# Expert products in scaled fp16 parts made once in the first stage, and single tiles in the pairs' form

## The chip, the core and the metric

One core of one Trainium2 chip runs the whole program. The metric is the device time of one execution in microseconds (us); less is better. The engines are named as the profile names them: PE is the matrix engine (PEld its weight loads), DVE the vector engine, ACT the scalar engine, POOL the general engine, SP the engine that issues most transfers.

## The reference

Four residual blocks over x (4 x 1024 tokens of 256 numbers): cross attention, a mixture of experts with a shared network, a second cross attention, and a gated network with integer weights. The change touches the second block alone:

```python
logits = (xt @ gate_w.T + gate_b).astype(jnp.float32)
scores = jax.nn.softmax(logits, axis=-1)
top_w, top_i = jax.lax.top_k(scores, TOPK)          # 2 of 8 experts for each token
...
def expert(w1e, b1e, w3e, b3e, w2e, b2e):           # each matrix is 256 x 256
    h = jax.nn.silu(xt @ w1e.T + b1e) * (xt @ w3e.T + b3e)
    return h @ w2e.T + b2e
outs = jax.vmap(expert)(w1, b1, w3, b3, w2, b2)
y = jnp.einsum('etd,te->td', outs, gate_dense)
z = jax.nn.silu(xt @ ws1.T + bs1) * (xt @ ws3.T + bs3) @ ws2.T + bs2
```

## The kernel before

**Three stages.** Stage 1 takes the tokens in 8 groups of 512. Its `step(g)` (g from 1 to 7, one on each engine) interleaves the first attention of group g with the shared network and the routing of group f = g - 1, and POOL scatters the normalised rows to DRAM by expert (`rows_by_expert`). Stage 2 (the expert loop) takes the scattered rows in 40 units: 31 pairs (256 rows) and 9 singles (128 rows), in the order of `KINDS`: 13 pairs, then nine times pair, pair, single. Stage 3 gathers the experts' results and does the rest of the shared network, the second attention and the last network. Nothing is scheduled by a planner: every engine runs the order written in its block, and semaphores tie them.

**Products in parts.** A product of full precision is three matmuls (`three`, L1306): high x high, high x low, low x high, where high is the value copied to the narrow type `F32R` on ACT and low is the rest, subtracted on DVE. The three stand in the profile at L1308, L1309 and L1310.

**Stage 2 before.** SP loads for each unit the two first matrices of its expert (`wraw`, 512 KB, L470), ACT copies them to `wph` (`weights_high`, L985) and DVE subtracts `wpl` (`weights_low`, L2272): once per unit, 40 times. The second matrices of all 8 experts (`w2h`, `w2l`) are split in stage 1 instead: in each step `expert_high(g)` on ACT (128x512, the last of the step; two of them in step 1) and `expert_low(g)` on DVE. PE transposes the unit's rows (`tx`, L1649), makes the hidden layer (`hidden`: for a pair the weights are stationary and 24 matmuls of 256 columns run; for a single the rows are stationary, 6 matmuls of 512 columns, and the hidden layer must be transposed back by `th`, L1686), and multiplies by the second matrix (`outp`, 12 or 6 matmuls of 256 columns). The order on PE for unit u is `hidden(u)`, `outp(u - 2)`, `th(u - 1)` where that is a single, `tx(u + 2)`. ACT does `silu_of`, `out_copy`, `rows_high`, `high_of`; DVE `gated`, `rows_low`, `hidden_low_of`; POOL adds the bias; SP stores.

**Stage 1, one step, in order.** PE: `up(f,0)`, `probs_t(g)`, setup products of the second attention (steps 2 to 6; in step 3 `queries`), `up(f,1)`, `values(g)`, `gate(f)`, `up(f,2)`, `gate_back`, `t1(g+1)`, `up(f,3)`, `scores(g+1)` (waits for both `n1T` copies), `rank`, `down(f)` first part, `t2(g)`, `down(f)` second part. ACT: `silu(f,0)`, `pt_copy(g)` (writes `probsT`, for which `values` waits), `silu(f,1)`, `hidden_high(f,0)`, `logit_copy`, `silu(f,2)`, `hidden_high(f,1)`, `t1_copy(g+1)` (writes `n1T`), `hidden_high(f,2)`, `ln2_apply(g)`, `silu(f,3)`, `hidden_high(f,3)`, `route_exp`, `t2_copy(g)` (`n2Th`, for which the next `up` waits), `softmax(g+1)`, `expert_high(g)`. DVE: `hidden(f,0)`, `residual1`, `ln2_stats`, `hidden(f,1)`, `route_a`, `hidden(f,2)`, `route_b`, `hidden(f,3)`, `route_d`, `row_max(g+1)`, `t2_low(g)`, `shared_out`, `ln1_stats`, `route_c`, `expert_low(g)`.

## Time and profile before

| | before |
|---|---|
| median of 3 runs | 618.06 us (617.78 to 622.72) |
| the profiled execution, its own time | 616.33 us |
| its span in the profile | 614.5 us |
| PE busy | 569.9 us, 93% |
| DVE busy | 453.1 us, 74% |
| ACT busy | 377.6 us, 61% |
| POOL busy | 253.5 us, 41% |
| granted PE clock, mean | 0.985 of full |
| moved by DMA | 93.15 MB, mean 152 GB/s |

The profile is one execution, and its 616.33 us stands 1.73 us under the median; 1.83 us of it lie outside the span. Matmuls are pipelined, so the duration of one (0.28 us for 256 columns) is not what it costs: the distance between two starts is. The chain of waits that ended last is PE for 66% of the span and DVE for 17%.

### The profile page before, as it was taken

How to read it: one execution, taken by the hardware profiler on the slowest of the kernel's cores; microseconds unless marked ns; L12 is line 12 of the kernel's file. 1: busy time of each engine (PE TensorE's matmuls, PEld its weight loads, DVE VectorE, ACT ScalarE, POOL GpSimd, SP SyncE). 2: the span in 40 equal slices, each digit the busy share in tenths (PEclk: the TensorE clock that was granted, in tenths of full speed). 3: DMA queues.
4: the chain of work that ended last, by engine and by line, in shares of the span. 5: the costliest groups of instructions: out<-in, count | busy, mean ns of one | idle time of the engine just before them, and what ended most of it. 6: DMA issues, size and time to landing. Idle time of an engine off the chain costs nothing.

```text
span 614.5 us, 12817 instructions
## 1 busy us (share of the span) xinstructions
PE 569.9 (93%) x3906; PEld 469.0 (76%) x3906; DVE 453.1 (74%) x1246; ACT 377.6 (61%) x729; POOL 253.5 (41%) x284
## 2 busy tenths in 40 slices
PE   7889999998967999999999999799889989999997
PEld 7788888886747999999999988476646646655654
DVE  5887887886644877778788863477888798877755
ACT  5576777873534777777687663155574674684643
POOL 4445665553540134454343345577533640410100
PEclk9899999998997999999999999999999999999999
DMA  7334664441238868887978717542212240200000
GB/s 213 120 112 143 206 207 161 153 166 58 104 137 249 284 223 287 276 248 249 311 225 291 240 67 285 186 157 69 62 35 70 85 138 35 69 2 35 34 36 35
DMA packets 46005, 93.15 MB, mean 152 GB/s; under 512 B 6686, under 2 KB 15978, under 8 KB 45682
## 3 DMA queue, kind: packets, MB, share of 16 engines
q1 hardware_dynamic: 37868, 74.34, 35.5%
q0 software_dynamic: 7344, 17.97, 9.7%
q8 instruction: 33, 0.54, 0.4%
q14 instruction: 34, 0.28, 0.1%
q10 hardware_dynamic: 726, 0.02, 0.1%
HBM read 61.32 MB, written 32.17 MB: 152 GB/s over the span
## 4 chain that ended last, share of the span: by engine, by line
PE 66%; DVE 17%; issue 6%; ACT 5%; another core or an unknown queue 4%; POOL 1%; DMA 0%; ACTq 0%; DVEq 0%; POOLq 0%
PE bank L1310 13%; PE bank L1308 13%; PE bank L1309 12%; PE bank L1805 6%; DVE st L2381 3%; PE bank L1649 2%; PE bank L1826 2%; PE bank L1827 2%; PE bank L1277 2%; PE bank L1294 2%; DVE g3l L2458 2%; DVE xa L2372 2%; DVE sl L2453 2%; PE bank L1266 1%
## 5 line engine op out<-in xcount | busy, mean ns | idle before, releaser
L625 POOL DMA_INDIRECT rows_by_expert<-n,pos x64 | 64.6, 1010 | 53.4 <-DVE pos L2109 36.9
L674 POOL TENSOR_TENSOR yg<-yg,b 128x512 f32<-128x512 f32 x31 | 44.7, 1443 | 98.6 <-ACT yg L798 98.6
L722 POOL DMA_INDIRECT yr<-expert_out,out_row x64 | 64.7, 1011 | 28.3 <-issue 19.7
L1308 PE MATMUL bank<-xTh,wph 128*128 128x256 f32 x248 | 73.8, 297 | 1.7 <-DVE xTl L2300 1.2
L1805 PE MATMUL bank<-m4Th,wint 128*128 128x512 f16 x192 | 69.0, 380 | 5.3 <-DVE sl L2453 3.3
L1310 PE MATMUL bank<-xTh,wpl 128*128 128x256 f32 x248 | 71.2, 287 | 0.0
L1309 PE MATMUL bank<-xTl,wph 128*128 128x256 f32 x248 | 71.1, 287 | 0.0
L1805 PE MATMUL bank<-m4Tl,wint 128*128 128x512 f16 x192 | 68.8, 379 | 0.0
L2274 DVE TENSOR_TENSOR wpl<-wraw,wph 128x1024 fp32r<-128x1024 f32 x40 | 49.0, 1225 | 12.8 <-ACT wph L798 12.6
L798 ACT ACTIVATE wph<-wraw 128x1024 fp32r<-128x1024 f32 x40 | 42.3, 1058 | 16.3 <-PE bank L1310 9.6
L1308 PEld LDWEIGHTS bank<-xTh,wph 128*128 128x128 f32 x248 | 48.5, 196 | 2.1 <-issue 1.4
L2453 DVE SCALAR_TENSOR_TENSOR sl<-bank,sl 128x512 f32<-128x512 f32 x48 | 33.0, 688 | 22.5 <-ACT sl L1113 22.4
L1309 PEld LDWEIGHTS bank<-xTl,wph 128*128 128x128 f32 x248 | 48.6, 196 | 0.0
L1310 PEld LDWEIGHTS bank<-xTh,wpl 128*128 128x128 f32 x248 | 48.5, 196 | 0.0
L1826 PE MATMUL bank<-wint,g3h 128*128 128x256 f16 x192 | 42.9, 273 | 1.3 <-DVE g3l L2458 0.8
L1113 ACT ACTIVATE sl<-bank 128x512 f32<-128x512 f32 x48 | 28.3, 589 | 25.2 <-PE bank L1805 24.5
L1827 PE MATMUL bank<-wint,g3l 128*128 128x256 f16 x192 | 42.8, 273 | 0.0
L1308 PE MATMUL bank<-w2h,hTh 128*128 x142 | 40.2, 283 | 1.4 <-DVE hTl L2330 1.4
L1066 ACT ACTIVATE n<-xa,nb,rs 128x256 f32<-128x256 f32 x64 | 34.1, 589 | 11.3 <-DVE nb L2398 10.9
L1805 PEld LDWEIGHTS bank<-m4Th,wint 128*128 128x128 f16 x192 | 18.3, 97 | 29.1 <-DVE sl L2453 7.9
L2310 DVE SCALAR_TENSOR_TENSOR hb<-bank,b13c,hb 128x256 f32<-128x256 f32 x62 | 27.1, 479 | 17.7 <-PE bank L1310 17.6
L1310 PE MATMUL bank<-w2h,hTl 128*128 x142 | 40.2, 283 | 0.0
(351 smaller groups left out, 1754.5 us busy)
## 6 DMA issues: line engine op xcount, KB each, us to landing
wraw<-in_wexp SPq DMA_DIRECT2D x40, 512.0 KB
xg<-rows_by_expert SPq DMA_DIRECT2D x31, 256.0 KB, 3.9
...
```

What stands on the lines that cost most here:

```text
L625: pool.indirect_dma_start(out=xs, out_offset=bass.IndirectOffsetOnAxis(ap=pos[p][:, k, j:j + 1], axis=0), in_=n2[p][:, j, :], in_offset=No ...
L674: pool.tensor_tensor(yg[u % 3], yg[u % 3], b2[:, bass.ds(e, 1), :].broadcast_to([P, 2, D]), ALU.add)\
L722: pool.indirect_dma_start(out=yr[:, c, k, j, :], out_offset=None, in_=ys, in_offset=bass.IndirectOffsetOnAxis(ap=out_row[:, b * GB + c, k, ...
L798: return act.activation(dst, src, ACT.Copy)
L1308: mm(o, ah, bh, start=first, stop=False)
L1309: mm(o, ah, bl, start=False, stop=False)
L1310: return mm(o, al, bh, start=False, stop=final)
L1805: last = mm(bank[:, 2 * (m % 2) + w, :], wt[:, k, m * P:(m + 1) * P], part[c][:, k, :], start=(q == 0 and k == 0), stop=(q == 1 and k == K ...
L1826: mm(bank[:, j, 0:D], g3h[:, k, t], wdv[:, k, :], start=(k == 0), stop=False)
L1827: last = mm(bank[:, j, 0:D], g3l[:, k, t], wdv[:, k, :], start=False, stop=(k == ML - 1))
L2274: tt(wpl[u % 2], wraw[u % 3], wph[u % 2], ALU.subtract).then_inc(sem("low_done0"), 1)
L2453: stt(sl3[n % 3], bank[:, 2 * (m % 2) + 1, :], HID_SCALE, sl3[n % 3], ALU.mult, ALU.mult).then_inc(sem("g3_done"), 1)
```

## The change

1. **Type.** All expert products take fp16 parts instead of `F32R` ones. fp16 needs a scale, so ACT squares and sums every weight (`weight_squares`, `bias_squares`), one small matmul adds over the partitions, and DVE derives six powers of two (`weight_scales`).
2. **Place.** All 24 matrices are loaded raw in stage 1 (`load_raw`: twice four transfers of 768 KB), split once (`weight_high` on ACT, `weight_low13` and `weight_low2` on DVE), and kept on chip in `w13q` and `w2q`. `load_weights`, `weights_high`, `weights_low`, `expert_high`, `expert_low` and the 2 MB broadcast of `b13` go.
3. **Singles** run in the pairs' form: weights stationary, 24 matmuls of 128 columns; `th` goes.
4. **Transposes** `tx` take `F32R` (`identr`).
5. **Waits.** The first tile load waits for the last split (`wq_low`), since the tiles lie where the raw weights were. `queries` (step 3) waits for the squares, and `up(2,2)` in step 3 waits until DVE has read their sums from the same bank. The activations of stage 2 take scales by pointer.

The core of the diff:

```diff
...
-        wraw = [wa.put(f"wraw{p}", [P, KD, 2 * F], F32) for p in range(3)]
-        wph = [wa.put(f"wph{p}", [P, KD, 2 * F], F32R) for p in range(2)]
-        wpl = [wa.put(f"wpl{p}", [P, KD, 2 * F], F32R) for p in range(2)]
-        wa.at = area_a + 2 * NE * KD * 2 * F * 4
-        w2h = wa.put("w2h", [P, NE, KD * D], F32R)
-        w2l = wa.put("w2l", [P, NE, KD * D], F32R)
+        w13q = wa.put("w13q", [P, NE, 2, KD * 2 * F], F16)
+        w2q = wa.put("w2q", [P, NE, 2, KD * D], F16)
+        area_r = wa.at
+        raw = wa.put("raw", [P, NE, 3, 512], F32)
...
-            def load_expert(e):
-                c = e % 3
-                sp.wait_ge(sem(f"low_done{c}"), e // 3 + 2)
-                src = i["wexp"][bass.ds(e * (3 * P) + 2 * P, P), :]
-                sp.dma_start(stage[c], src).then_inc(sem(f"stage_in{c}"), 16)
+            def load_raw(h):
+                for e in range(4 * h, 4 * h + 4):
+                    src = i["wexp"][e * (3 * P):(e + 1) * (3 * P), :].rearrange("(a p) n -> p a n", p=P)
+                    sp.dma_start(raw[:, e, :, :], src).then_inc(sem(f"raw_in{h}"), 16)
...
-            load_expert(0)
-            load_expert(1)
             for dst, src in ((wk.rearrange("p k j -> p (k j)"), "wk"), (wv.rearrange("p k j -> p (k j)"), "wv"),
                              (wqT, "wqT"), (wo.rearrange("p k j -> p (k j)"), "wo"), (bqk, "bqk"), (bvr, "bv")):
                 small(dst, i[src], "l1_in")
             small(b13r, i["b13"], "l1_in")
+            load_raw(0)
             step(1, 1)
...
-            sp.wait_ge(sem("table_done"), 1)
-            load_weights(0)
+            sp.wait_ge(sem("wq_low"), 2 * NE)
             sp.wait_ge(sem("table_done"), 3)
...
+            def weight_squares(e):
+
+                act.wait_ge(sem(f"raw_in{e // 4}"), 64)
+                act.activation(w13q[:, e % 4, 0, :], raw13[e], ACT.Square, accum_out=ssq[:, e:e + 1])\
+                    .then_inc(sem("bound_step"), 1)
+                act.activation(w2q[:, e % 4, 0, :], raw[:, e, 2, :], ACT.Square, accum_out=ssq[:, NE + e:NE + e + 1])\
+                    .then_inc(sem("bound_step"), 1)
+
+            def bias_squares():
+                act.wait_ge(sem("filled"), 1)
+                act.wait_ge(sem("l1_in"), 16 * 7)
+                act.activation(w2q[0:NE, 0, 1, :], b13r, ACT.Square, accum_out=ssq[0:NE, 2 * NE:2 * NE + 1])\
+                    .then_inc(sem("bound_step"), 1)
+
+            def weight_high(e):
+                if e == 0:
+                    act.wait_ge(sem("filled"), 1)
+                    act.wait_ge(sem("bound_step"), 2 * NE + 5)
+                if e >= 5:
                     act.wait_ge(sem("setup_copied"), 8)
                     act.wait_ge(sem("l1_out"), 64)
-                stage_high(g % 3, w2h[:, g, :], g // 3 + 3)
+                act.activation(w13q[:, e, 0, :], raw13[e], ACT.Identity, bias=zeros[:, 0:1], scale=w13_scale).then_inc(sem("wq_high"), 1)
+                act.activation(w2q[:, e, 0, :], raw[:, e, 2, :], ACT.Identity, bias=zeros[:, 0:1], scale=w2_scale)\
+                    .then_inc(sem("wq_high"), 1)
...
                 hidden_high(f, 0)
                 logit_copy(f)
+                if g < 3:
+                    weight_squares(4 * g - 4)
                 silu(f, 2)
                 hidden_high(f, 1)
+                if g < 3:
+                    weight_squares(4 * g - 3)
+                if 4 <= g < 7:
+                    weight_high(2 * g - 7)
                 if nxt:
                     t1_copy(g + 1, ks=(0,))
...
+                if g < 3:
+                    weight_squares(4 * g - 2)
...
-                expert_high(g)
+                if g < 3:
+                    weight_squares(4 * g - 1)
+                if g == 2:
+                    bias_squares()
+                if g >= 3:
+                    weight_high(min(2 * g - 6, NE - 1))
...
+                act.activation(xTh[u % 2][:, 0:n], bank[:, 4 + u % 2, 0:n], ACT.Copy, scale=ROW_SCALE).then_inc(sem("xTh_done"), 1)
...
+                act.activation(hTh[u % 2][:, 0:n], hb[u % 2][:, 0:n], ACT.Identity, bias=zeros[:, 0:1], scale=h_scale)\
+                    .then_inc(sem("hTh_done"), 1)
...
+                if m == 2 and f == 2:
+                    pe.wait_ge(sem("bound_step"), 2 * NE + 4)
...
+                pe.wait_ge(sem("bound_step"), 2 * NE + 1)
+                mm(bank[:, piece_bank(2, 1), 408:408 + 2 * NE + 1], mean_of, ssq, start=True, stop=True).then_inc(sem("bound_step"), 1)
...
-                        last = pe.transpose(bank[:, 4 + u % 2, at:at + P], xg[u % 4][:, j, k * P:(k + 1) * P], ident)
+                        last = pe.transpose(bank[:, 4 + u % 2, at:at + P].bitcast(F32R), xg[u % 4][:, j, k * P:(k + 1) * P], identr)
...
-                pe.wait_ge(sem("low_done0"), EARLY[0] + u + 1)
+            def hidden(u, e):
+
+                p, w = u % 2, width(u)
                 pe.wait_ge(sem("xTl_done"), u + 1)
-                if u >= 2 and pair(u - 2):
-                    pe.wait_ge(sem("h2_done"), 2 * (tile_slot(u - 2) + 1))
-                elif u >= 2:
-                    pe.wait_ge(sem("hb_done"), tile_slot(u - 2) - NP + 1)
-                if pair(u):
-                    for m in range(4):
-                        o = bank[:, 2 * p + m // 2, m % 2 * P2:(m % 2 + 1) * P2]
-                        for k in range(KD):
-                            wh, wl = (w[p][:, k, m * P:(m + 1) * P] for w in (wph, wpl))
-                            n = slice(k * P2, (k + 1) * P2)
-                            last = three(o, wh, wl, xTh[p][:, n], xTl[p][:, n], k == 0, k == KD - 1)
-                        if m == 1:
-                            last.then_inc(sem("ha_done"), 1)
-                else:
+                if u >= 2:
+                    pe.wait_ge(sem("h2_done"), 2 * (u - 1))
+                for m in range(4):
+                    o = bank[:, 2 * p + m // 2, m % 2 * P2:m % 2 * P2 + w]
                     for k in range(KD):
-                        s = slice(k * P, (k + 1) * P)
-                        last = three(bank[:, 2 * p, :], xTh[p][:, s], xTl[p][:, s], wph[p][:, k, :], wpl[p][:, k, :],
-                                     k == 0, k == KD - 1)
+                        s = slice(k * 2 * F + m * P, k * 2 * F + (m + 1) * P)
+                        wh, wl = (w13q[:, bass.ds(e, 1), q, s].rearrange("p a n -> p (a n)") for q in range(2))
+                        n = slice(k * w, (k + 1) * w)
+                        last = three(o, wh, wl, xTh[p][:, n], xTl[p][:, n], k == 0, k == KD - 1)
+                    if m == 1:
+                        last.then_inc(sem("ha_done"), 1)
                 last.then_inc(sem("hm_done"), 1)
-
-            def th(u):
-                p = u % 2
-                pe.wait_ge(sem("hid_done"), tile_slot(u) - NP + 1)
-                pe.wait_ge(sem("y_done"), u - 1)
-                for k in range(KD):
-                    last = pe.transpose(bank[:, 6 + p, (KD + k) * P:(KD + k + 1) * P], hb[p][:, k * P:(k + 1) * P], ident)
-                last.then_inc(sem("th_done"), 1)
...
-            def expert_low(g):
-                low_part(g % 3, w2h[:, g, :], w2l[:, g, :], g // 3 + 3)
+            def weight_low13(e):
+                dve.wait_ge(sem("wq_high"), 2 * e + 1)
+                stt(w13q[:, e, 1, :], raw13[e], w13_scale, w13q[:, e, 0, :], ALU.mult, ALU.subtract).then_inc(sem("wq_low"), 1)
+
+            def weight_low2(e):
+                dve.wait_ge(sem("wq_high"), 2 * e + 2)
+                stt(w2q[:, e, 1, :], raw[:, e, 2, :], w2_scale, w2q[:, e, 0, :], ALU.mult, ALU.subtract).then_inc(sem("wq_low"), 1)
...
+            def weight_scales():
+
+                dve.wait_ge(sem("bound_step"), 2 * NE + 2)
+                dve.wait_ge(sem("setup_copied"), 5)
+                sums = bank[:, piece_bank(2, 1), 408:408 + 2 * NE + 1]
+                dve.tensor_reduce(bound[:, 0:2], sums[:, 0:2 * NE].rearrange("p (q e) -> p q e", q=2), AX.X, ALU.max)\
+                    .then_inc(sem("bound_step"), 1)
+                cp(bound[:, 2:3], sums[:, 2 * NE:2 * NE + 1]).then_inc(sem("bound_step"), 1)
...
                 hidden(f, 1)
+                if g == 3:
+                    weight_scales()
                 route_a(f)
                 route_a2(f)
                 hidden(f, 2)
                 hidden_low(f, 1)
+                if g >= 4:
+                    weight_low2(2 * g - 8)
                 route_b(f)
                 hidden_low(f, 2)
                 hidden(f, 3)
+                if 4 <= g < 7:
+                    weight_low13(2 * g - 7)
+                    weight_low2(2 * g - 7)
...
-                if g == 1:
-                    expert_low(0)
-                expert_low(g)
+                if g >= 3:
+                    weight_low13(min(2 * g - 6, NE - 1))
...
+            weight_low2(NE - 1)
             route_c(f)
...
```

**Where instructions now stand.** ACT in step 4, from the second `hh` of the step (`hidden_high(3,1)`) on, before; `n1T` are the two copies for which `scores(5)` waits on PE:

```order
L861 ACTIVATE sil_123<-bank,bs_57 128x256
L798 ACTIVATE hh<-sil_124 128x256
L798 ACTIVATE n1T<-bank 128x512 x2
L798 ACTIVATE hh<-sil_123 128x256
L815 ACTIVATE n_119<-x_117,nb_140,rstd_138 128x256 x2
```

and in the change (`w13q`, `w2q` are the parts kept on chip, `raw` the loaded weights):

```order
L867 ACTIVATE sil_127<-bank,bs_58 128x256
L785 ACTIVATE hh<-sil_128 128x256
L812 ACTIVATE w13q<-raw,zeros,scale_i 128x1024
L813 ACTIVATE w2q<-raw,zeros,scale_i 128x512
L785 ACTIVATE n1T<-bank 128x512 x2
L785 ACTIVATE hh<-sil_127 128x256
```

The split of one expert stands between `hh` and `n1T`, in steps 4, 5 and 6; in steps 1 and 2 a pair of squares stands there. A second such pair stands at the end of each step in the place of `expert_high` (128x512). DVE in step 3 from `hidden(2,1)` on, before:

```order
L2033 SCALAR_TENSOR_TENSOR sil_124<-bank,bs_57,sil_124 128x256
L2049 TENSOR_TENSOR logit<-bank,gbias 128x32
L2051 TENSOR_TENSOR logit<-bank,logit 128x32
L2054 MAX top_143<-logit 128x8 x4
L2057 MAX_INDEX top8i<-top_143,logit 128x8 x4
```

and in the change, cut after the first nine:

```order
L2050 SCALAR_TENSOR_TENSOR sil_128<-bank,bs_58,sil_128 128x256
L1940 TENSOR_REDUCE bound<-bank 128x2
L1942 COPY bound<-bank 128x1
L1944 TENSOR_SCALAR bound<-bound 128x3
L1946 TENSOR_SCALAR bound_e_75<-bound 128x3
L1947 TENSOR_SCALAR bound_e_76<-bound_e_75 128x3
L1948 TENSOR_SCALAR bound_e_77<-bound_e_76 128x3
L1949 CAST bound_f<-bound_e_77 128x3
L1950 TENSOR_SCALAR bound_f<-bound_f 128x1
```

The sums are read after `hidden(2,1)`, and sixteen small instructions stand ahead of the routing's first. PE at the start of `hidden` for the first unit, before (four transposes of the unit after it stand ahead):

```order
L1649 MATMUL bank<-ident,xg_179 128x128 x4
L1308 MATMUL bank<-xTh_180,wph_98 128x256
L1309 MATMUL bank<-xTl_182,wph_98 128x256
L1310 MATMUL bank<-xTh_180,wpl_100 128x256
L1308 MATMUL bank<-xTh_180,wph_98 128x256
```

and in the change, for the second unit:

```order
L1653 MATMUL bank<-identr,xg_181 128x128 x4
L1308 ISA
L1308 MATMUL bank<-xTh_184,w13q 128x256
L1309 MATMUL bank<-xTl_186,w13q 128x256
L1310 ISA
L1310 MATMUL bank<-xTh_184,w13q 128x256
L1308 ISA
```

The weights are now addressed by the expert's number, and two register instructions (`ISA`) go with every three matmuls of `hidden`.

## Rows read from the trace of the kernel before

**Rows 1.** The first two stages: stretch, length, busy us (instructions), PEclk, DMA

```profile
0.00:194.63 194.63, 172.62 (x1238) 151.61 (x1239) 142.57 (x624) 119.03 (x261) 96.17 (x126) 0.97 0.46 152
194.63:368.67 174.04, 172.25 (x1377) 169.46 (x1377) 134.49 (x198) 124.60 (x228) 67.54 (x59) 0.98 0.76 247
```

**Rows 2.** Timeline of PE, one pair: start, duration, engine, line, operation, count

```profile
231.82 0.60 PE L1649 MATMUL bank<-ident,xg 128*128 128x128 f32 x4
...
236.57 0.60 PE L1649 MATMUL bank<-ident,xg 128*128 128x128 f32 x4
236.93 0.36 PE L1308 MATMUL bank<-xTh,wph 128*128 128x256 f32 x1
237.13 0.28 PE L1309 MATMUL bank<-xTl,wph 128*128 128x256 f32 x1
...
239.76 0.28 PE L1310 MATMUL bank<-xTh,wpl 128*128 128x256 f32 x1
```

**Rows 3.** Timeline of PE, first and last matmul of a single's hidden layer

```profile
361.85 0.40 PE L1308 MATMUL bank<-wph,xTh 128*128 128x512 f32 x1
...
363.01 0.39 PE L1310 MATMUL bank<-wph,xTl 128*128 128x512 f32 x1
```

**Rows 4.** Timeline of PE, stage 3, fp16 parts, 13 distances apart

```profile
461.14 0.27 PE L1826 MATMUL bank<-wint,g3h 128*128 128x256 f16 x1
...
462.56 0.27 PE L1827 MATMUL bank<-wint,g3l 128*128 128x256 f16 x1
```

**Rows 5.** Timeline of SP, then PE, first tiles of stage 2 [idle before]

```profile
186.85 1.46 SPq L462 DMA_DIRECT2D xg<-rows_by_expert  x2
...
192.32 1.08 PE L1649 MATMUL bank<-ident,xg 128*128 128x128 f32 x8 [2.40 <-issue]
194.63 0.55 PE L1308 MATMUL bank<-xTh,wph 128*128 128x256 f32 x1 [1.23 <-DVE xTl L2300]
```

**Rows 6.** Timeline of PE, last product of stage 2

```profile
367.84 0.39 PE L1308 MATMUL bank<-w2h,hTh 128*128 x1 [1.35 <-DVE hTl L2330]
```

**Rows 7.** Timeline of ACT, then PE, step 4

```profile
91.02 1.07 ACT L798 ACTIVATE n1T<-bank 128x512 f32<-128x512 f32 x2
...
99.72 0.65 ACT L798 ACTIVATE w2h<-stage 128x512 fp32r<-128x512 f32 x1
...
92.15 0.67 PE L1277 MATMUL bank<-ctxC,n1T 128*128 128x77 f32 x4 [0.29 <-ACT n1T L798]
```

**Rows 8.** Groups by line and form, ACT: busy us, mean ns, idle before

```profile
L798 ACT ACTIVATE wph<-wraw 128x1024 fp32r<-128x1024 f32 x40 | 42.3, 1058 | 16.3 <-PE bank L1310 9.6 <-DMA wraw<-in_wexp 6.4
...
L815 ACT ACTIVATE n<-x,nb,rstd 128x256 f32<-128x256 f32 x32 | 17.3, 589 | 1.6 <-POOL nb L613 1.0 <-DMA rows_by_expert<-n,pos 0.7
...
L798 ACT ACTIVATE hh<-sil 128x256 fp32r<-128x256 f32 x24 | 9.9, 411 | 5.4 <-DVE sil L2033 4.2 <-issue 1.0
```

**Rows 9.** Timeline of PE, then DVE, step 3

```profile
69.75 0.28 PE L1308 MATMUL bank<-n2Th,wsh 128*128 128x256 f32 x1
...
72.11 0.48 DVE L2033 SCALAR_TENSOR_TENSOR sil<-bank,bs,sil 128x256 f32<-128x256 f32 x1
```

**Rows 10.** Timeline of SP, ACT and PE, step 1

```profile
23.83 0.33 SPq L357 DMA_DIRECT2D b13r<-in_b  x1
...
34.64 0.47 ACT L861 ACTIVATE sil<-bank,bs 128x256 f32<-128x256 f32 x1 [2.93 <-DVE hl L1947]
...
36.44 0.67 PE L1277 MATMUL bank<-ctxC,n1T 128*128 128x77 f32 x4 [1.51 <-ACT n1T L798]
```

**Rows 11.** Stretches in steps 7 and 1, columns as in rows 1

```profile
147.24:149.07 1.83, 0.00 (x1) 0.01 (x1) 1.80 (x9) 0.62 (x2) 1.30 (x1) 0.95 0.00 0
149.07:152.30 3.23, 3.23 (x8) 2.56 (x9) 3.16 (x23) 1.76 (x5) 0.38 (x2) 0.50 0.00 0
...
36.44:40.00 3.56, 3.56 (x37) 3.54 (x38) 2.80 (x16) 3.19 (x8) 0.00 (x0) 1.00 0.00 0
...
20.00:23.00 3.00, 1.46 (x11) 1.49 (x12) 2.93 (x9) 0.03 (x1) 2.82 (x5) 0.93 0.97 323
```

199 lines of the change are left out of this document (77 added, 122 removed).

## The prediction

> **What bounds the kernel now.** I read the three stages first, in the stretches of the program. In stage 1 (194.63 us) PE is busy 172.6 us, and in stage 2 (174.04 us) 172.25 us, against 134.5 for DVE and 124.6 for ACT [rows 1]. So stage 2 is bound by PE outright: there each nanosecond less for a matmul counts, and ACT and DVE have 40 to 50 us to spare. In stage 1 PE is the busiest too, but it is tied to ACT inside each step. The timeline of step 4 shows how closely: ACT begins the `n1T` copies at 91.02, right behind its other work, and PE waits 0.29 us for them before `scores` at 92.15 [rows 7]. Work of ACT put ahead of `n1T` is paid by PE at once, less whatever PE had still to do.
>
> **Stage 2, the type.** In a pair's `hidden`, the 22 distances between the starts at 237.13 and 239.76 make 0.1195 us for 256 columns of `F32R` [rows 2]. In stage 3 fp16 parts of the same size stand 0.1092 us apart (13 distances from 461.14 to 462.56) [rows 4]. Difference 0.0103. A pair has 24 + 12 such matmuls and a single 6 (`outp`): 31 x 36 + 9 x 6 = 1,170, so 12.1 us are gained. After the four f32 transposes the first product takes 0.20 (236.93 to 237.13) [rows 2] instead of 0.12; with `identr` and fp16 I take 0.065 of that 0.08 as gone, for 40 units: 2.6.
>
> **Transposes.** 142 of `tx` at 0.09 (four in the 0.36 from 236.57 to 236.93 [rows 2]). No row has one in `F32R` with its cost by itself. Bounds: half of the 256-column distance, 0.055, and no gain, 0.09; I take the middle, 0.0725: 2.5 us (0 to 5). `th` goes: 18 at 0.09, 1.6.
>
> **Singles.** Before, 6 matmuls of 512 columns, 0.232 apart (361.85 to 363.01 in five) [rows 3], 54 in all: 12.6 us. After, 216 of 128 columns, whose distance no row shows. Half of 0.109 is the lower bound (11.8), the 0.09 of a transpose of 128 columns with its own weight load the upper (19.4). I take 0.0625, since the 512-column distance scales down to it and the weight load stands beside the matmul: 13.5, a loss of 0.9 (gain 0.7, loss 6.9). The Trainium skill speaks against this part of the change: "TensorE: Matmul & The Clock Gate", section "Back-to-back issue gap", gives a stream of weight load and matmul a sustained spacing of about 81 ns at 128 columns. By that, called an estimate, the singles would take 17.5 us and lose 4.9 instead of 0.9. No row of this kernel has that stream.
>
> **The ends of stage 2.** The last product waits 1.35 us for `hTl` [rows 6]; the chain of a single is now the shorter one of a pair, so I give 1.0 back. At the start the tiles were issued at 186.85 and PE began `tx` at 192.32 and `hidden` at 194.63 [rows 5]; each of those tiles lay behind 512 KB of first matrices, which are no longer loaded, and I take 1.4 us of it. The cover on ACT and DVE grows: `wph`, 1,058 ns for each unit [rows 8], and the subtraction are gone, while two pointers on an activation cost 589 - 411 = 0.178 us for 256 columns [rows 8]. Their sum per unit falls, so PE stays the bound. **Sum of stage 2: 12.1 + 2.6 + 2.5 + 1.6 - 0.9 + 1.0 + 1.4 = 20.3 us gained,** 12 to 27 by the bounds.
>
> **Stage 1, what one split costs ACT.** `weight_high(e)` is 1024 and 512 columns: 1.06 [rows 8] + 0.65 (`w2h` in [rows 7]) + 2 x 0.178 for the pointers = 2.06. Neighbouring copies overlap (the two `n1T` take 1.07 together, not 2 x 0.65 [rows 7]), which takes 0.23 off: 1.83 us. A pair of squares is taken at the same 1.8. Before, ACT had one such 0.65 in a step. Total ACT work added: 8 squares and 8 splits, 29 us, less 5.
>
> **Steps 4 to 6.** A split between `hidden_high(f,1)` and `t1_copy` moves `n1T` back by 1.83, and PE has nothing else in its order than `scores`. ACT makes part of it good (it waited there for DVE and PE), so that `n2Th`, for which the next step's first `up` waits, is 1.6 late; the split at the end is 1.83 where `w2h` was 0.65, 1.16 more, ahead of the next `silu` and `probsT`. 2.8 a step, 8.3 in all. DVE's `weight_low` work fits under PE and POOL, as DVE has 52 us free in stage 1 [rows 1].
>
> **Step 3.** `up(2,2)` begins at 69.75 now, and DVE ends `hidden(2,1)` at 72.11 + 0.48 = 72.59 [rows 9]. It has to wait until DVE has then read the sums from the same bank (two small instructions): about 73.0, 3.25 us. Queued behind it on PE are `gate_back`, `t1`, `up(2,3)` and `scores(4)`, so nothing fills the gap. With the end's 1.16: 4.4.
>
> **Steps 1, 2 and 7.** `load_raw(0)` is 3.146 MB issued behind `b13r` (23.83 [rows 10]). At the 323 GB/s of the stretch 20 to 23 [rows 11] it needs 9.7 us: landed near 34, first squares done near 35.9. ACT's `silu` at 34.64, after 2.93 of idle [rows 10], is then 1.3 late, and the second squares add 1.8 before `n1T`: `scores`, which waits 1.51 there already [rows 10], starts 3.1 later. With what is left of the two pairs behind it the step is 5.0 longer (3.4 to 9: the upper end if the loads share the queues with the first tokens and weights). Step 2 has its raw weights in time: one pair fits in ACT's idle, the others and `bias_squares` add 1.8 + 0.55 + 1.15 + 0.6 = 4.1. Step 7 has no middle insertion, only the last split: 0.5.
>
> **The clock.** PE's idle of 1.83 us at 147.24 is followed by a granted clock of 0.50 for 3.23 us, all of it busy [rows 11]; that level is 1.2 GHz, half of 2.4. The other idles of this length in the trace of before are followed by it as well, but the 1.51 of step 1 is not: 1.00 behind it [rows 10, 11]. A fall costs half of 3.23, 1.6 us. Steps 1 and 3 make idles of over 3 us: two falls, 3.2. In steps 2, 4, 5 and 6 the new idle is 1.83 + 0.29 = 2.1, close to the edge: I count half of the four, 3.2.
>
> **Sum of stage 1: 5.0 + 4.1 + 4.4 + 8.3 + 0.5 + 6.4 = 28.7 us lost.** Stage 3 keeps its instructions and only shifts. Against the profiled execution: 616.33 + 28.7 - 20.3 = 624.7; its own time is 1.73 below the median, which I don't add, since single runs differ by that. **Forecast 625 us.**
>
> **Rivals.** (1) *Slower, the sum above*, 0.45: for it speaks that every insertion stands ahead of something PE is seen to wait for. Its own range is 620 to 634. (2) *No change, 612 to 624*, 0.35: the same mechanism, but idles of 2.1 us bring no fall (-3.2), and transposes or singles come out at their lower bounds (-2.5, -1.7): 617. ACT's 0.29 tie in step 4 speaks against more than that. (3) *Faster, the other side*, 0.2: ACT pays the middle split back out of its idle before `n2Th`, so that a step of 4 to 6 costs 1.2 (-4.8), the same in step 2 (-1.8), and there are no falls (-6.4): 611.7; it decides once steps 4 to 6 cost under 1.5 us each and stage 1 as a whole under 14. For it speaks that ACT is busy in only 119 of 194.6 us [rows 1]; against it, that the idle lies where ACT waits for PE's own products, which are late as well. (4) *Stage 2 gives little*, inside the 0.45: the register instructions that stand among the matmuls, or 128 columns at 0.09, hold PE back. At 0.09, 6.0 more than I take, it ends at 631; it would also reach the bound of 12 us for stage 2, 633. (5) *The change's type does nothing*: if fp16 with stationary parts changed at each matmul stood at 0.1195, as `F32R` does, 12.1 more: 637. Rows 4 are the same form in stage 3, so I give it under 0.05.
>
> **How the numbers follow.** About 1% (6 us) is what a measurement of this kernel can tell from no change: faster is below 612, slower above 624. (1), (4) and (5) together give slower 0.45, (2) same 0.35, (3) faster 0.20. The range 610 to 634 leaves out the part of (3) in which the gain of stage 2 is at its upper bound as well, and the upper tail of step 1 with (5).
>
> **What would show it.** In stage 2: starts of `hidden` 0.109 apart (0.1195 would make the type worth nothing), singles with 24 matmuls in about 1.5 us, a length near 155 us instead of 174, and PE still waiting for nobody. In stage 1: `hidden(0)` on PE beginning near 222 instead of 194.63; PE's wait for `n1T` near 2 us in steps 4 to 6, a wait of over 3 us ahead of the third `up` of step 3, and ACT's first squares waiting for the raw weights until about 34. The granted clock at 0.50 after the waits of steps 1 and 3. The prediction is wrong in its size if ACT takes back the middle splits before `n2Th` (steps 4 to 6 longer by 1.2 and not 2.8), if the raw weights land after 36, or if the split of expert 5 waits for the stores of the first block, whose completion it needs in step 6; and in its sign if stage 1 grows by less than 14 us.

## The result and the profile after

| | before | after |
|---|---|---|
| median of 4 runs | 618.11 us (617.78 to 622.72) | 628.14 us (626.43 to 636.79) |
| the profiled execution, its own time | 616.33 us | 626.43 us |
| its span | 614.5 us | 624.7 us |
| stage 1 (to the first product of stage 2) | 194.63 us | 223.22 us |
| stage 2 (first product to last) | 173.9 us | 155.6 us |
| granted PE clock, mean | 0.985 | 0.959 |

The ratio of after to before is 1.0145, 95% interval 1.010 to 1.019: the change makes the kernel slower. Times of one kernel spread by several us from run to run here, so every experiment below is compared with the runs of the kernel before that were made beside it. The ratios leave out runs over 1.5% above the fastest of their kernel; the medians keep them.

The stages of after, to hold against [rows 1] (stretch, length, then busy us and instructions of PE, PEld, DVE, ACT and POOL, then PEclk, DMA share, GB/s; the third is stage 3):

```profile
0.00:223.22 223.22, 185.58 (x1241) 161.98 (x1241) 155.66 (x650) 141.06 (x301) 97.65 (x127) 0.90 0.44 149
223.22:378.95 155.73, 153.33 (x1521) 137.85 (x1521) 87.94 (x159) 107.71 (x198) 57.44 (x59) 0.99 0.43 132
378.95:624.70 245.75, 226.76 (x1294) 149.02 (x1292) 176.13 (x424) 134.33 (x241) 90.73 (x100) 0.99 0.25 84
```

Stage 2 is 18.3 us shorter, stage 3 is as long as before (245.8), stage 1 is 28.6 us longer. The row of stage 1 splits that growth in two. PE has the work of before and a few small matmuls, yet it is busy 185.58 us instead of 172.62: 13.0 us more, because the granted clock is 0.90 instead of 0.97. The rest, 15.6 us, is idle: 37.6 instead of 22.0. So nearly half of what stage 1 lost is not a wait but work at a lower clock.

PE's waits in after, the largest groups (what waited, for whom, us in total, times, longest):

```profile
PE bank L1277 <- ACT n1T L785: 12.2, 5, 5.7
PE bank L1294 <- ACT probsT L785: 4.3, 3, 1.6
```

Before, PE waited for `n1T` 1.51 us in step 1 and 0.29 in step 4 [rows 7, 10]. Where the waits stand, and what became of the clock, is in PE's timeline. The starts of `scores` and the idle before them:

```profile
40.02 1.14 PE L1277 MATMUL bank<-ctxC,n1T 128*128 128x77 f32 x4 [5.71 <-ACT n1T L785]
...
63.03 0.67 PE L1277 MATMUL bank<-ctxC,n1T 128*128 128x77 f32 x4 [1.61 <-ACT n1T L785]
...
111.96 0.33 PE L1277 MATMUL bank<-ctxC,n1T 128*128 128x77 f32 x1 [1.83 <-ACT n1T L785]
...
134.48 1.13 PE L1277 MATMUL bank<-ctxC,n1T 128*128 128x77 f32 x4 [2.13 <-ACT n1T L785]
...
158.85 0.67 PE L1277 MATMUL bank<-ctxC,n1T 128*128 128x77 f32 x4 [0.88 <-ACT n1T L785]
```

Four matmuls take 0.67 us in step 2, at the full clock, and 1.14 and 1.13 in steps 1 and 5, at the half clock: the records themselves tell it. Stretches of step 1 and step 3 in after, columns as above, to hold against [rows 11]:

```profile
34.31:40.02 5.71, 0.00 (x1) 0.01 (x1) 2.62 (x23) 5.10 (x13) 0.68 (x2) 0.89 1.05 409
40.02:45.72 5.70, 5.70 (x33) 5.64 (x34) 2.27 (x11) 5.68 (x12) 0.30 (x1) 0.51 0.70 271
76.00:82.60 6.60, 6.59 (x20) 4.20 (x19) 2.65 (x8) 1.74 (x6) 2.90 (x3) 0.53 0.25 87
82.60:84.73 2.13, 0.00 (x1) 0.03 (x1) 2.06 (x13) 0.59 (x1) 0.95 (x1) 0.50 0.75 246
84.73:90.00 5.27, 5.27 (x25) 5.01 (x26) 3.46 (x31) 1.38 (x3) 0.49 (x2) 0.50 0.01 3
```

In step 3 the half clock begins before the wait for the sums (82.60 to 84.73), and lasts on through it to 90. That is nearly 14 us at 1.2 GHz instead of 2.4, 11.5 of them busy, in the step that the prediction priced at one fall of 1.6. It is not the only long one: stage 1 of after has stretches at half clock in steps 4 and 6 as well (113 to 117 and 152 to 155), a longer one in step 5, and the longest but one near its end, where before has 3.5 us (183 to 186.5). The last two:

```profile
134.60:141.20 6.60, 6.60 (x38) 6.54 (x39) 4.59 (x14) 4.28 (x9) 1.16 (x1) 0.50 0.00 0
206.00:216.30 10.30, 7.49 (x32) 6.41 (x32) 5.28 (x15) 3.24 (x5) 0.96 (x1) 0.50 0.24 78
```

Stage 2 in PE's timeline, two pairs and then a single with the start of `outp` behind it, to hold against [rows 2] and [rows 3]:

```profile
251.50 0.54 PE L1653 MATMUL bank<-identr,xg 128*128 128x128 f32 x4
...
255.74 0.54 PE L1653 MATMUL bank<-identr,xg 128*128 128x128 f32 x4
...
307.33 0.23 PE L1308 MATMUL bank<-xTh,w13q 128*128 128x128 f16 x1
307.40 0.22 PE L1309 MATMUL bank<-xTl,w13q 128*128 128x128 f16 x1
...
308.63 0.22 PE L1310 MATMUL bank<-xTh,w13q 128*128 128x128 f16 x1
309.04 0.28 PE L1308 MATMUL bank<-w2q,hTh 128*128 x1 [0.20 <-issue]
```

A pair takes 4.24 us (255.74 - 251.50) instead of 4.75. A single's 24 matmuls of 128 columns stand 0.056 apart (22 distances from 307.40 to 308.63). Behind them PE idles for 0.20 us, ended by "issue": it waited for no engine.

The other idles of PE in after that are spoken of below, at the start of step 1, ahead of the sums in step 3, and at both ends of stage 2, to hold against [rows 5] and [rows 6]:

```profile
21.69 0.36 PE L1308 MATMUL bank<-n2Th,wsh 128*128 128x256 f32 x1 [1.84 <-DVE n2Tl L2021]
...
74.04 0.37 PE L1451 MATMUL bank<-ssq,mean_of 128*128 128x17 f32 x2 [1.42 <-ACT w2q L802]
...
221.03 0.87 PE L1653 MATMUL bank<-identr,xg 128*128 128x128 f32 x8 [1.75 <-issue]
...
378.27 0.28 PE L1308 MATMUL bank<-w2q,hTh 128*128 x1 [1.43 <-DVE hTl L2337]
```

And ACT's first squares in step 1, an idle of 3.83 us for the raw weights ahead of them:

```profile
34.92 1.06 ACT L794 ACTIVATE w13q<-raw 128x1024 f16<-128x1024 f32 x1 [3.83 <-DMA raw<-in_wexp]
35.88 0.19 ACT L794 ACTIVATION_READ_ACCUMULATOR w13q<-raw 128x1 f32 x1
```

### The profile page after: what moved, and what is told of

Read it like the earlier page. It is cut to its first block, busy times and chain, and to the rows that moved or that the text cites. A ratio compares the mean times of both kernels' runs of the same rounds, so it can differ in the third digit from the quotient of the medians.

```text
span 624.7 us, 13525 instructions
## 1 busy us (share of the span) xinstructions
PE 565.7 (91%) x4052; PEld 448.9 (72%) x4052; DVE 419.7 (67%) x1232; ACT 383.1 (61%) x740; POOL 245.8 (39%) x285
## 4 chain that ended last, share of the span: by engine, by line
PE 51%; DVE 20%; ACT 11%; issue 9%; another core or an unknown queue 4%; DMA 3%; POOL 1%; SPq 1%; ACTq 0%; DVEq 0%; POOLq 0%
PE bank L1308 10%; PE bank L1309 10%; PE bank L1310 10%; PE bank L1791 6%; DVE st L2377 3%; PE bank L1812 3%; PE bank L1813 2%; DVE g3l L2454 2%; DVE xa L2368 2%; PE bank L1653 2%; PE bank L1277 2%; DMA raw<-in_wexp 2%; DVE sl L2449 2%; ACT probs L841 1%
## 5 line engine op out<-in xcount | busy, mean ns | idle before, releaser
L1308 PE MATMUL bank<-xTh,w13q 128*128 128x256 f16 (+1 forms) x320 | 81.3, 264 | 1.3 <-DVE xTl L2320 1.3
L1309 PE MATMUL bank<-xTl,w13q 128*128 128x256 f16 (+1 forms) x320 | 80.9, 263 | 0.0
L1310 PE MATMUL bank<-xTh,w13q 128*128 128x256 f16 (+1 forms) x320 | 80.9, 263 | 0.0
L661 POOL TENSOR_TENSOR yg<-yg,b 128x512 f32<-128x512 f32 x31 | 39.5, 1275 | 98.3 <-ACT yg L1043 98.3
L2320 DVE SCALAR_TENSOR_TENSOR xTl<-bank,xTh 128x512 f16<-128x512 f32 (+1 forms) x40 | 25.2, 631 | 51.5 <-ACT xTh L1017 51.5
L1043 ACT ACTIVATE yg<-bank,zeros,scale_i 128x512 f32<-128x512 f32 (+1 forms) x40 | 29.2, 730 | 44.9 <-PE bank L1310 44.9
L1308 PE MATMUL bank<-w2q,hTh 128*128 x142 | 38.8, 273 | 2.4 <-DVE hTl L2337 1.4
L2330 DVE SCALAR_TENSOR_TENSOR hb<-bank,b3s,hb 128x256 f32<-128x256 f32 (+1 forms) x80 | 32.8, 450 | 12.2 <-ACT hb L1026 6.0
L1308 PE MATMUL bank<-n2Th,wsh 128*128 128x256 f32 (+1 forms) x104 | 36.3, 350 | 4.1 <-issue 2.1
L785 ACT ACTIVATE g3h<-sl 128x512 f16<-128x512 f32 x48 | 30.0, 626 | 16.2 <-DVE sl L2449 15.9
L1026 ACT ACTIVATE hb<-bank,b13c,scale_i 128x256 f32<-128x256 f32 (+1 forms) x80 | 38.8, 539 | 0.0
L1309 PE MATMUL bank<-w2q,hTh 128*128 x142 | 38.8, 273 | 0.0
```

What stands on the lines that cost most here:

```text
L661: pool.tensor_tensor(yg[u % 3], yg[u % 3], b2[:, bass.ds(e, 1), :].broadcast_to([P, 2, D]), ALU.add)\
L1026: act.activation(hb[u % 2][:, m * w:(m + 1) * w], bank[:, 2 * (u % 2), m * P2:m * P2 + w], ACT.Silu, bias=b13c[:, m:m + 1, bass.ds(e, 1)]. ...
L1308: mm(o, ah, bh, start=first, stop=False)
L1309: mm(o, ah, bl, start=False, stop=False)
L1310: return mm(o, al, bh, start=False, stop=final)
```

## The experiments

In the table are the starts of `scores` for steps 1 to 6 and of the first product of stage 2, read from PE's timeline of each profiled run. A difference between neighbours is a step. The last column is the median less that of the kernel before beside it. The starts are those of one execution; for e1 it is the slowest of its four (635.96 us).

| | 1 | 2 | 3 | 4 | 5 | 6 | stage 2 | median, us | to before |
|---|---|---|---|---|---|---|---|---|---|
| before | 36.44 | 55.37 | 74.09 | 92.15 | 110.60 | 129.12 | 194.63 | 618.11 | |
| after | 40.02 | 63.03 | 91.36 | 111.96 | 134.48 | 158.85 | 223.22 | 628.14 | +10.0 |
| e1, wait later | 43.43 | 67.53 | 95.03 | 116.88 | 137.91 | 160.15 | 231.18 | 628.17 | +8.6 |
| e2, middle splits in a gap | 40.31 | 63.82 | 90.61 | 109.38 | 129.13 | 149.95 | 214.60 | 620.29 | +0.7 |
| e3, no squares | 35.92 | 56.20 | 74.71 | 98.21 | 119.01 | 142.81 | 212.69 | 618.62 | -1.0 |
| e5, fillers too long | 44.92 | 66.16 | 89.83 | 111.69 | 133.62 | 154.34 | 218.14 | 626.88 | +10.9 |
| e6, moved to gaps | 35.92 | 56.21 | 78.52 | 98.31 | 119.33 | 139.58 | 202.40 | 605.57 | -10.4 |
| e9, fillers halved | 39.24 | 60.61 | 87.35 | 107.95 | 128.96 | 149.66 | 212.80 | 618.48 | -0.2 |
| e10, e1 and e2 | 40.33 | 63.79 | 87.73 | 109.00 | 128.39 | 148.25 | 211.73 | 614.80 | -3.9 |

The theory to begin with: stage 1 grows because squares and splits stand on ACT ahead of what PE waits for, and the idle brings the half clock. The rival: ACT's added work must be paid somewhere, wherever it stands. A second rival: the half clock is a symptom, hidden in waits for ACT.

### e1: the wait for the sums one product later

```diff
-                if m == 2 and f == 2:
+                if m == 3 and f == 2:
                     pe.wait_ge(sem("bound_step"), 2 * NE + 4)
```

> The changed kernel with one wait moved: in step 3 the third product up(2,2) no longer waits until DVE has read the sums; the fourth, up(2,3), does, which is the one that writes the same bank. Theory (the wait in front of up(2,2) costs because gate_back, t1 and up(2,3) queue behind it): the idle of 2.14 us before up(2,2) goes, DVE gets gate_back's result earlier, and the time falls by 2 to 4 us, part of it by a shorter stretch at half clock. Rival (DVE reads the sums so late that only the place of the wait moves): PE waits about 2 us ahead of up(2,3) instead, and the time is the same within 1 us.

Measured: 628.17 us (623.08 to 635.96), the time of after within its spread; ratio to before 1.013 (1.007 to 1.018). PE from `values` of step 3 to the next `scores`, in after and then in e1:

```profile
77.27 3.62 PE L1294 MATMUL bank<-ctxr,probsT 77*128 77x256 f32 x8
...
91.36 0.56 PE L1277 MATMUL bank<-ctxC,n1T 128*128 128x77 f32 x4
```

```profile
84.48 3.62 PE L1294 MATMUL bank<-ctxr,probsT 77*128 77x256 f32 x8
...
95.03 0.56 PE L1277 MATMUL bank<-ctxC,n1T 128*128 128x77 f32 x4
```

The way is 10.6 us instead of 14.1 (7.0 before: 67.10 to 74.09), and no wait stands ahead of `up(2,3)`. The trace speaks for the theory, the time doesn't decide: its runs lie 13 us apart, and the gain looked for is 2 to 4. e10 below does.

### e2: the middle splits moved into a gap of ACT

```diff
                 logit_copy(f)
                 if g < 3:
                     weight_squares(4 * g - 4)
+                if 4 <= g < 7:
+                    weight_high(2 * g - 7)
                 silu(f, 2)
                 hidden_high(f, 1)
                 if g < 3:
                     weight_squares(4 * g - 3)
-                if 4 <= g < 7:
-                    weight_high(2 * g - 7)
```

> The changed kernel with the middle split of steps 4, 5 and 6 moved on ACT from behind the second hh to ahead of the third silu, where ACT waits 1.7 to 2.0 us for DVE in the trace of the changed kernel. Nothing is added or left out. Theory (the place costs, not the work): PE's waits for n1T in steps 4 to 6 (1.83, 2.13 and 0.88 us) go, and with them the half clock behind the second (6 us of it, 3 us lost); the time falls by 5 to 9 us. Rival (ACT is full in these steps and pays elsewhere): silu, hh and n1T come as late as before and the time is the same within 1.5 us.

Measured: 620.29 us over 10 runs (616.18 to 623.90), 0.7 above before instead of 10.0: 9.3 us came back, just over the upper end of what the theory said. Steps 4 to 6 take 59.3 us (90.61 to 149.95) instead of 67.5. ACT in step 5 of e2:

```profile
124.71 0.59 ACT L785 ACTIVATE logitT<-bank 16x512 f32<-16x512 f32 x1 [1.93 <-PE bank L1416]
125.20 1.23 ACT L812 ACTIVATE w13q<-raw,zeros,scale_i 128x1024 f16<-128x1024 f32 x1
126.34 0.80 ACT L813 ACTIVATE w2q<-raw,zeros,scale_i 128x512 f16<-128x512 f32 x1
127.33 0.48 ACT L867 ACTIVATE sil<-bank,bs 128x256 f32<-128x256 f32 x1 [0.19 <-DVE hl L1964]
127.70 0.41 ACT L785 ACTIVATE hh<-sil 128x256 fp32r<-128x256 f32 x1
128.01 1.07 ACT L785 ACTIVATE n1T<-bank 128x512 f32<-128x512 f32 x2
```

The split of 2 us fills what was an idle of 2.03 us ahead of `silu`; there is still 0.19 left. The same instructions cost 9 us less in this place. They may still cost something: steps 4 to 6 took 55.0 us in before. That ACT is full falls as a rival.

### e3: no squares

```diff
-                if g < 3:
-                    weight_squares(4 * g - 4)
...
-                mm(bank[:, piece_bank(2, 1), 408:408 + 2 * NE + 1], mean_of, ssq, start=True, stop=True).then_inc(sem("bound_step"), 1)
...
+                chained(dve.memset(bound, 4.0))
```

> The changed kernel without the squares of weights and biases, without the small matmul that adds them and without the read of the sums; the bound on the weights is a constant instead, so this part of the computation is left out. All splits stay where they are. Theory (steps 1 to 3 grew by 3.6, 4.1 and 9.6 us through the squares, the wait for the raw weights and the read of the sums, with the half clock they bring): 17.3 less the 1.2 of the split at the end of step 3 come back, so 14 to 18 us. Rival (the 6.3 MB of raw weights slow the first loads and the steps by themselves, or later steps take the gain back): under 8 us.

Measured: 618.62 us over 10 runs, from 609.25 to 622.17, 1.0 below before: 11 us came back, between what the theory and the rival said. Its ratio to before, without its five slowest runs, is 0.989 (0.986 to 0.992), 7 us below; by that 16 came back, as the theory said. So the size is not settled closer than 11 to 16 us. Steps 1 to 3 returned as said: `scores` of step 3 starts at 74.71 instead of 91.36, where before has 74.09. So the raw loads by themselves cost steps 1 to 3 less than 1 us. But from there to stage 2 the profiled run takes 138.0 us against 131.9 in after, with the same instructions. The end of that part in e3 and after, columns as above:

```profile
142.81:212.69 69.88, 57.36 (x339) 46.86 (x340) 40.48 (x151) 31.77 (x56) 25.72 (x26) 0.90 0.28 93
```

```profile
158.85:223.22 64.37, 54.43 (x340) 44.55 (x340) 40.32 (x152) 31.79 (x56) 26.42 (x26) 0.92 0.31 108
```

Half of the 5.5 us more is PE busy longer on the same work (57.4 against 54.4), at a lower clock. That falls of the clock, at the middle and end splits still in place, are what spreads e3 over 13 us is likely and not shown: one of its runs was profiled.

### e4: the type alone, in the kernel before

```diff
-        wph = [wa.put(f"wph{p}", [P, KD, 2 * F], F32R) for p in range(2)]
+        wph = [wa.put(f"wph{p}", [P, KD, 2 * F], F16) for p in range(2)]
...
-        xTh = [ct.put(f"xTh{p}", [P, KD * P2], F32R) for p in range(2)]
+        xTh = [ct.put(f"xTh{p}", [P, KD * P2], F16) for p in range(2)]
```

(and so for `wpl`, `w2h`, `w2l`, `xTl`, `hTh`, `hTl`)

> The kernel before with one thing changed: the parts of the expert products are fp16 instead of F32R, without scales (so small low parts lose bits). Place, singles, transposes and loads are those of before. Theory (a 256-column matmul at 0.109 us instead of 0.1195, 1,170 of them, and PE bound throughout stage 2): stage 2 shortens by 12 to 15 us, the time falls to 603 to 606 us. Rival (ACT's and DVE's split of a unit's first matrices then sets the pace, or the distance doesn't change with the type): stage 2 shortens by under 6 us.

Measured: 611.79 us (609.43 to 613.49), 7.8 below before; ratio 0.990 (0.986 to 0.993). Stage 2 took 162.4 us instead of 173.9, 11.5 less, just under the 12 to 15 that were expected, and the 603 to 606 us were missed. PE had two waits in stage 2 that before has not, 1.2 us for a tile and 0.9 for DVE's `wpl`, so a little of the rival is there. The whole time fell by less than the stage did: in the profiled run stage 1 was 1.9 us longer (196.52 instead of 194.63). Two pairs in PE's timeline of e4:

```profile
230.15 0.60 PE L1651 MATMUL bank<-ident,xg 128*128 128x128 f32 x4
...
234.51 0.60 PE L1651 MATMUL bank<-ident,xg 128*128 128x128 f32 x4
```

A pair takes 4.36 us: the type gives 0.39 of the 0.51 us that a pair gains in all.

### e5 and e9: matmuls that do nothing in PE's waits

```diff
+            def fill(n):
+                for _ in range(n):
+                    mm(bank[:, 6, KV:P], ident, ident[:, KV:P], start=True, stop=True)
...
                 if nxt:
+                    fill((22, 5, 0, 6, 7, 3)[g - 1])
                     scores(g + 1, bn)
```

(the counts of e9; also 4 ahead of `values` in steps 4 to 6, and 4 and 6 in step 3)

> The changed kernel with matmuls that do nothing (f32, 51 columns, into columns of bank 6 that nobody reads) put on PE ahead of the waits of stage 1: 45, 12, 13, 13 and 7 ahead of scores in steps 1, 2, 4, 5, 6, 9 ahead of values in steps 4 to 6, 10 and 12 in step 3. Each bunch is sized to end before what PE waits for. Nothing of the computation is changed. Theory (the idle costs twice: once as a wait, once as the half clock behind it, 15.4 us of lost speed in stage 1 of the changed kernel's trace): the stretches at half clock between 38 and 155 us go, the waits stay, and the time falls by 8 to 14 us, with a smaller spread between runs. Rival (at full clock PE is only earlier at the next wait for ACT, which sets the pace): the waits grow by what the clock gives, and the time is the same within 2 us.

Measured: 626.88 us (two runs at 622, two at 632 and 633): the 8 to 14 us did not come. The premise of the size was wrong: a filler took 0.22 us, so PE ended step 1's bunch 4.5 us after `n1T` was there, and no wait over 0.3 us was left in steps 1 to 6. Still, in the profiled run, one of the two at 622, the granted clock was 1.00 from 27 to 203 us, and stage 1 was 5 us shorter than in after with all that added. Halved:

> As the run with 45, 12, 13 and so on matmuls that do nothing, with half as many (22, 5, 6, 7, 3 ahead of scores, 4 ahead of values, 4 and 6 in step 3), since one of them took 0.22 us and not the 0.10 assumed, so that the bunches ended after what PE waited for (by 4.5 us in step 1, by 0.6 to 1 in steps 2, 4 and 5). Theory (the half clock is a cost of its own, about 15 us of stage 1): no stretch at half clock between 38 and 155 us, stage 1 ends 9 to 12 us sooner than the 223.2 of the changed kernel, the time is 614 to 619 us. Rival (ACT sets the pace, the clock is hidden in the waits): 625 us and above, with PE's waits for n1T and probsT grown.

Measured: 618.48 us over 10 runs (615.60 to 621.78), 0.2 below before instead of 10.0 above: 10 us came back with every square and split in its place. Stage 1 ends 10.4 us sooner. Stretches of e9, columns as above:

```profile
36.00:46.00 10.00, 9.57 (x90) 9.27 (x89) 4.14 (x19) 9.97 (x23) 2.67 (x3) 1.00 0.88 336
46.00:75.00 29.00, 27.43 (x206) 24.20 (x207) 20.02 (x89) 27.15 (x69) 15.63 (x18) 1.00 0.46 154
75.00:85.50 10.50, 10.50 (x44) 8.60 (x43) 6.79 (x36) 1.79 (x5) 3.37 (x4) 0.51 0.25 87
85.50:155.00 69.50, 65.69 (x542) 60.96 (x540) 60.10 (x255) 55.45 (x114) 34.47 (x37) 1.00 0.39 131
```

One stretch at half clock was left between 36 and 155 us, in step 3, where the expectation said none. PE was busy through all its 10.5 us (fillers stood in the wait for the sums), and the last idle ahead of it was one of 0.61:

```profile
71.62 0.37 PE L1455 MATMUL bank<-ssq,mean_of 128*128 128x17 f32 x2 [0.61 <-ACT w2q L802]
```

The second rival falls: waits did not grow by what the clock gave (the largest left for `n1T` is 1.21 us, in step 6). The half clock is a cost of its own, 10 us of it measured here by time and 13 by PE's busy time in after.

### e10: e1 and e2 together

> The changed kernel with the middle splits of steps 4 to 6 ahead of the third silu and the wait for the read of the sums ahead of up(2,3) instead of up(2,2). Against the run with the first of these alone (620.3 us): theory (the wait ahead of up(2,2) held gate_back, t1 and up(2,3) back; in the trace of the run that moved it alone, the way from values to scores of step 3 was 10.6 us instead of 14.1) 2 to 4 us less, 616 to 618 us. Rival (it is hidden by the half clock or paid back): the same 620 within 1 us.

The edit is the diffs of e1 and e2. Measured: 614.80 us (613.47 to 616.91), 3.9 below before, where e2 was 0.7 above: 4.6 us for the wait, a little over what was expected; ratio to before 0.993 (0.989 to 0.996), against 1.001 (0.997 to 1.005) for e2. In its profiled run the way from `values` to `scores` in step 3 is 10.1 us (77.63 to 87.73) and has no idle, in that of e2 12.95 (77.66 to 90.61) with the wait of 2.14. This settles what e1 alone left open: the wait costs time. The rest of the 4.6 the traces don't place.

### e6: squares and splits moved to gaps of ACT

```diff
                 hidden_high(f, 0)
+                if 1 < g < 4:
+                    weight_squares(3 * g - 5)
+                if g >= 5:
+                    weight_high(2 * g - 9)
                 logit_copy(f)
-                if g < 3:
-                    weight_squares(4 * g - 4)
+                if 1 < g < 4:
+                    weight_squares(3 * g - 4)
+                if g >= 5:
+                    weight_high(2 * g - 8)
                 silu(f, 2)
                 hidden_high(f, 1)
...
-                if m == 2 and f == 2:
+                if m == 3 and f == 3:
                     pe.wait_ge(sem("bound_step"), 2 * NE + 4)
```

(squares of experts 0, 3, 6 and 7 and splits of 0 and 7 stand late in steps or at their ends; the sums go to step 4, and DVE's halves of the splits move a step later with ACT's)

> The changed kernel with all squares and splits kept, but placed where ACT waits in its trace: ahead of logit_copy and ahead of the third silu. Squares of experts 1, 2 in step 2 and 4, 5 in step 3, of 0 and 3 at the ends of steps 1 and 2, of 6 and 7 late in step 3; the sums are added in step 4 into another bank, for which up(3,3) waits; splits from the end of step 4 on, two in each of steps 5 to 7, the last at the end of step 7. Theory (place, not work): step 1 returns to the 20.6 us of before, steps 2 to 7 cost 1 to 2 us each where a split or squares still stand at an end, stage 1 grows by 8 to 12 us instead of 28.6, the time is 606 to 611 us, faster than both kernels. Rival (ACT's added work of 24 us net must be paid somewhere): over 618 us.

Measured: 605.57 us (604.24 to 606.17); ratio to before 0.982, 0.976 to 0.987. It computes all that the changed kernel computes, and is 10 us below the kernel before and 20 below the changed one, just under what was expected. Several moves are in it together, and the 20 us are of all of them. ACT in step 5 of e6:

```profile
113.20 1.24 ACT L812 ACTIVATE w13q<-raw,zeros,scale_i 128x1024 f16<-128x1024 f32 x1
114.33 0.81 ACT L813 ACTIVATE w2q<-raw,zeros,scale_i 128x512 f16<-128x512 f32 x1
115.23 0.59 ACT L785 ACTIVATE logitT<-bank 16x512 f32<-16x512 f32 x1
115.72 1.23 ACT L812 ACTIVATE w13q<-raw,zeros,scale_i 128x1024 f16<-128x1024 f32 x1
116.86 0.80 ACT L813 ACTIVATE w2q<-raw,zeros,scale_i 128x512 f16<-128x512 f32 x1
```

Stage 1 of e6, columns as above:

```profile
0.00:202.40 202.40, 176.96 (x1241) 152.84 (x1241) 154.27 (x649) 140.64 (x301) 99.08 (x127) 0.96 0.47 160
```

ACT does 140.6 us of work in stage 1, as in after (141.1), and stage 1 is 20.8 us shorter: 7.8 over before, where 8 to 12 were expected. Idle of PE is 25.4 us (22.0 before, 37.6 after), and PE's busy time 177.0 (172.6 and 185.6). Its runs spread over 2 us, those of after over 10.

### e7 and e8: the small terms of stage 2

```diff
-        xg = [ct.put(f"xg{p}", [P, 2, D], F32R) for p in range(4)]
+        xg = [ct.put(f"xg{p}", [P, 2, D], F32) for p in range(4)]
...
-                        last = pe.transpose(bank[:, 4 + u % 2, at:at + P].bitcast(F32R), xg[u % 4][:, j, k * P:(k + 1) * P], identr)
+                        last = pe.transpose(bank[:, 4 + u % 2, at:at + P], xg[u % 4][:, j, k * P:(k + 1) * P], ident)
```

> The changed kernel with the transposes of the tiles back in f32; all else is kept. Only the length of stage 2 (155.6 us from the first product to the last in the changed kernel) is read. Theory of the prediction (a transpose costs 0.0725 instead of 0.09, and what follows it starts sooner): stage 2 is 2.5 to 5 us longer. Rival (the type of the transposes does nothing, the shorter first product comes from fp16): the same within 0.5 us.

Measured, in one run: stage 2 took 158.0 us instead of 155.6, all of it at the full clock, where after ran the first 3.3 us at half and lost 1.6. So the difference is between 2.4 and 4.0: the theory holds. A pair in e7:

```profile
249.97 0.60 PE L1653 MATMUL bank<-ident,xg 128*128 128x128 f32 x4
...
254.34 0.60 PE L1653 MATMUL bank<-ident,xg 128*128 128x128 f32 x4
```

4.37 against 4.24 us: 0.13 for four transposes, 0.03 for one. e8:

```diff
-                        wh, wl = (w13q[:, bass.ds(e, 1), q, s].rearrange("p a n -> p (a n)") for q in range(2))
+                        wh, wl = (w13q[:, u % NE, q, s] for q in range(2))
```

> The changed kernel with the weights of stage 2 addressed by a constant (unit number modulo 8) instead of the expert in a register, so that the register instructions among the matmuls go; units are multiplied by the wrong expert's weights. Only the length of stage 2 is read. Theory (PE falls behind at the singles only, where it idles 0.20 us ahead of outp because the instructions of 24 short matmuls come too slowly): stage 2 is 1.5 to 3 us shorter than 155.6. Rival (that idle is a wait for another engine): the same within 0.5 us.

Measured, in one run: stage 2 took 152.8 us, 2.8 less, with its start at half clock as in after. The end of a single's `hidden` and the start of `outp` in e8:

```profile
302.94 0.22 PE L1310 MATMUL bank<-xTh,w13q 128*128 128x128 f16 x1
303.00 0.27 PE L1308 MATMUL bank<-w2q,hTh 128*128 128x256 f16 x1
```

0.06 us between the two instead of the 0.41 of after (308.63 to 309.04); pairs kept their 4.24. So the register instructions cost 0.3 us at each of the nine singles and nothing at the pairs, whose longer matmuls cover them.

## Why the prediction was right, and where its terms were off

The forecast of 625 us, slower, met 628.14: sign and place are right, and the mechanism too, work of ACT ahead of what PE waits for. That the size came out so near is in part luck: the terms beneath the sum were off, and some of them cancelled.

- **Stage 2** was to be near 155 us long; it is 155.6. A pair was worked out at 4.75 - 36 x 0.0103 - 0.065 - 4 x 0.0175 = 4.24, and takes 4.24. Within that, e4 and e7 divide it otherwise: 0.39 instead of 0.44 for type and first product, and 0.13 instead of 0.07 for four transposes. The wait at the end did not shrink: 1.43 us instead of 1.35 [rows 6], where 1.0 was given back.
- **Singles**: 216 matmuls at 0.056 take 12.1 us and not 13.5. What the prediction named only within rival (4), the register instructions, is real, but costs 2.8 us and only here. So the new form takes 14.9 us in all and the old, with `th`, 14.2 (54 at 0.232 are 12.5, not 12.6). The 81 ns that the Trainium skill gives ("TensorE: Matmul & The Clock Gate", "Back-to-back issue gap") is not what this stream shows; the measured 56 ns decides.
- **Start of stage 2**: 1.4 us was to be gained there; PE's idle ahead of `tx` is 1.75 us instead of 2.40 [rows 5], so 0.65 was.
- **Step 1** was right. ACT's squares waited for the raw weights until 34.92, said was about 34; `scores` came 3.6 us later, said was 3.1. e3 shows that it is the squares.
- **Step 3**: the wait for the sums was put at 3.25 us and is 2.13, and e10 gives 4.6 us for it in time. Why it costs more than itself is not shown; it lies in a stretch at half clock. The step as a whole grew by 9.6 us, where 4.4 and a fall of 1.6 had been said.
- **Steps 4 to 6** were to cost 8.3 us in waits and grew by 12.5 (2.5, 4.1 and 5.9). PE's idle in them grew by 6.4 (9.15 us instead of 2.75), its busy time on the same work by 6.1 (58.3 instead of 52.3), so the waits were put too high and the clock too low. The `n1T` waits are 1.83, 2.13 and 0.88 us, said was 2; but before has 0.69 and 0.92 of it in steps 5 and 6, not the 0.29 of step 4, so the wait did not grow in step 6. The waits for `probsT`, behind the split at a step's end, are 1.33, 1.33 and 1.65; no run moved the end splits by themselves. e2 returns 8.2 us of it by the place of three splits alone. The mechanism of rival (3), that ACT pays the middle split back later, is refuted by it.
- **The clock** is the mis-sized term: 6.4 us was said, PE's busy time shows 13.0, and e9 returned 10. Against that the waits cost 15.6 us, where the sum without the clock had 20.9 (22.3 less 1.4). Two errors of 5 to 7 us in opposite directions made the total of 27.3 look as good as it does against the 28.6 measured. The failed step is "a fall costs half of 3.23". It took one fall for each idle, of one length. In after the stretches at half clock in steps 1, 3, 4, 5 and 6 have 5.7, 11.5, 3.8, 6.6 and 3.2 us of busy time. That a further idle within one, as the wait for the sums in step 3, keeps it going is not shown: in e9 PE was busy throughout and the stretch of step 3 was 10.5 us long. And the rule that idles of 1.8 us or more bring a fall and shorter ones don't was read from five idles. In after 1.42 us ahead of the small matmuls of `queries` was followed by the longest one, while 1.61 us ahead of `scores` in step 2 and 1.84 at 21.7 were followed by none. The length of an idle by itself does not tell.

What stays open is which idle brings a fall. e8 runs the stage 1 of after unchanged, and after the same wait of 1.84 us at the start of step 1 (at 21.7) the clock fell in e8 and not in after. After, then e8:

```profile
21.70:27.00 5.30, 4.88 (x35) 4.33 (x36) 4.82 (x12) 3.62 (x12) 1.64 (x4) 1.00 0.89 274
```

```profile
21.70:27.00 5.30, 5.22 (x32) 5.25 (x32) 4.92 (x12) 2.75 (x11) 1.73 (x4) 0.68 0.85 261
```

So it varies from run to run with the same waits. Busy waits kept the clock at 1.00 from 27 to 203 us in e5, and in e9 from 36 to 155 us but for step 3.
